# Attention and expert layer on one core: the rotary affine moved behind the rotation, and the prologue reordered

## The reference, cut to what matters

```python
xn = x / jnp.maximum(norm, EPS) * g
uv = jax.nn.silu(xn @ uv_w.T)
u, v, base = uv[..., :E], uv[..., E:2 * E], uv[..., 2 * E:]
base = base[:, :, None, :] * gamma[None, None] + beta      # two rows: q and k
base = _rope_seq(base)    # concat([x1*cos - x2*sin, x2*cos + x1*sin]) over halves of 64
q, k = base[:, :, 0], base[:, :, 1]
qk = jnp.einsum('bis,bjs->bij', q, k) + w_rel[idx][None]
kernel = jnp.square(jax.nn.relu(qk / sqrt_s))
out = u * jnp.einsum('bij,bje->bie', kernel, v)
```

## Time and profile before

| | us |
|---|---|
| median of the runs | 323.87 |
| the three runs | 323.11, 326.44, 323.87 |
| the profiled execution | 326.97 |
| its span (first to last instruction) | 323.7 |
| TensorE busy in the span | 311.1 (96%) |
| VectorE, ScalarE, GpSimd busy | 239.1, 219.7, 190.2 |
| mean granted TensorE clock | 0.989 of full |

### The profile page before, as it was taken

How to read it: one execution, slowest core, us unless ns; L and a number is a source line. 1 busy time by engine, 2 the same in 40 slices (tenths; PEclk the granted TensorE clock), 3 DMA queues, 4 the chain that set the end, 5 groups by cost and what they waited for, 6 DMA issues and landing times.

```text
span 323.7 us, 7700 instructions
## 1 busy us (share of the span) xinstructions
PE 311.1 (96%) x2041; PEld 249.8 (77%) x2041; DVE 239.1 (74%) x776; ACT 219.7 (68%) x439; POOL 190.2 (59%) x190
## 2 busy tenths in 40 slices
PE   8969799999999999999999899999999999999996
PEld 7736365665758566575747899988999999999995
DVE  4770838988897888889898778996455545487766
ACT  2739538588586858756164677768888888698751
POOL 5471607048687787848565577787775455455440
PEclk9979989999999999999999999999999999999999
DMA  6993420002111110211115313323333222573744
GB/s 185 275 287 118 139 67 25 7 0 69 33 49 48 38 42 25 67 34 57 43 40 127 77 58 115 104 82 110 107 105 89 77 70 75 182 244 98 231 129 130
DMA packets 40972, 31.20 MB, mean 96 GB/s; under 512 B 5675, under 2 KB 36960, under 8 KB 40932
## 3 DMA queue, kind: packets, MB, share of 16 engines
q1 hardware_dynamic: 35472, 21.88, 24.6%
q0 software_dynamic: 4192, 8.44, 7.4%
q10 hardware_dynamic: 1268, 0.40, 0.6%
HBM read 16.95 MB, written 11.88 MB: 89 GB/s over the span
## 4 chain that ended last, share of the span: by engine, by line
PE 68%; DVE 9%; DMA 8%; ACT 6%; issue 6%; SPq 1%; ACTq 0%; POOL 0%; DVEq 0%; POOLq 0%
PE B_o L884 16%; PE B_o L954 13%; PE B_uv L943 12%; PE B_S L866 6%; PE B_o L893 4%; DMA y<-u,xb 3%; ACT s_rel L666 3%; PE B_uv L856 3%; PE B_uv L848 3%; DVE K L1381 2%; PE B_m L909 2%; PE B_xT L840 2%; DVE t L1162 1%; DMA v<-y 1%; PE B_xT L832 1%
## 5 line engine op out<-in xcount | busy, mean ns | idle before, releaser
L578 POOL DMA_INDIRECT y<-u,xb x67 | 67.3, 1005 | 43.0 <-ACT u L708 32.8
L954 PE MATMUL B_o<-W2s,K 128*128 x568 | 75.9, 277 | 2.2 <-DVE K L1381 1.3
L537 POOL DMA_INDIRECT slots<-rows,pos x64 | 66.3, 1036 | 18.1 <-issue 17.2
L954 PEld LDWEIGHTS B_o<-W2s,K 128*128 128x128 f32 x568 | 69.0, 192 | 4.0 <-issue 3.8
L884 PE MATMUL B_o<-K,v 128*128 128x512 f32 x128 | 60.4, 607 | 0.0
L884 PEld LDWEIGHTS B_o<-K,v 128*128 128x128 f32 x128 | 23.8, 196 | 21.8 <-issue 21.3
L866 PE MATMUL B_S<-qk 128*128 128x512 f32 x64 | 35.4, 637 | 3.4 <-DVE qk L1176 2.4
L943 PE MATMUL B_uv<-xbT,t 128*128 128x128 f32 x288 | 38.0, 275 | 0.0
L697 ACT ACTIVATE t<-W1s 128x644 f32 x36 | 26.5, 739 | 13.9 <-DVE yd L1387 12.7
L943 PEld LDWEIGHTS B_uv<-xbT,t 128*128 128x128 f32 x288 | 35.0, 192 | 0.5 <-issue 0.5
L1381 DVE TENSOR_TENSOR K<-B_uv,t 128x512 f32<-128x512 f32 x36 | 24.7, 688 | 13.3 <-PE B_uv L943 13.1
(11 more groups left out here) (238 smaller groups left out, 642.7 us busy)
## 6 DMA issues: line engine op xcount, KB each, us to landing
xb<-slots SPq DMA_DIRECT2D x71, 65.0 KB, 1.9
x_all<-L_attn_x SPq DMA_DIRECT2D x8, 256.0 KB, 3.1
W1s<-L_ffn_W SPq DMA_DIRECT2D x1, 2048.0 KB, 9.1
rows<-rows SPq DMA_DIRECT2D x8, 256.0 KB, 2.6
x_all<-y SPq DMA_DIRECT2D x4, 512.0 KB, 4.5
out<-acc SPq DMA_DIRECT2D x7, 256.0 KB
y<-u,xb POOLq DMA_INDIRECT x67, 2.4
slots<-rows,pos POOLq DMA_INDIRECT x64, 2.3
```

The source lines that it names most:

```text
L537: pool.indirect_dma_start(out=slots, out_offset=bass.IndirectOffsetOnAxis(ap=pos[:, q % 2, c:c + 1], axis=0), in_=rows[:, q % 2, c // T, c ...
L578: pool.indirect_dma_start(out=y2, out_offset=bass.IndirectOffsetOnAxis(ap=xb[:, k, D:D + 1].bitcast(u32), axis=0), in_=yb[:, k, :], in_off ...
L954: last = nc.tensor.matmul(B_y[n % 2], hT[:, n % 2, c * P:(c + 1) * P], W2s[:, bass.ds(w + c * D, D)], start=(c == 0), stop=(c == T - 1))
```

## The change

The affine is taken through the rotation. With R(x) = near(x)*cos + far(x)*sin, where far swaps the halves of 64 features and the sign lies in the table: R(gamma*base + beta) = gamma * (base*cos) + gamma_far * (base_far*sin) + (beta*cos + beta_far*sin). The last term depends on no batch.

- ScalarE writes `base2` with two planes, the silu of `B_xT` and the silu of `B_xT` with halves swapped (two instructions of 64x512), straight out of PSUM; `scale_base` is gone. Batch 0 signals its first plane by itself (`base_ready`).
- VectorE makes `rope_beta` once (`far_affine`, `beta_sin`, `beta_cos`: two small copies and four instructions of 128x512). Per batch it does one product of both planes with `rope_tab`, whose planes are the two tables (128x1024), and four scalar_tensor_tensor of 128x512 (`rope_near`, `rope_far`), which take gamma as a per-partition scalar. GpSimd's share in batch 0 is gone; there `first_rope` does the product in two halves, the near part while ScalarE still writes the swapped plane.
- SyncE loads both tables, in two DMAs, ahead of `W2` of expert 0 and of x(1).
- `rs1` and `mr1` have two buffers, so that `ln1_pow(b)` and `ln1_apply(b)` wait for z of batch b - 2 instead of b - 1.
- In the prologue: `first_mean` after `weights_low`; `bias_window` ahead of `ln1_stats(1)`, both after the rotation of batch 0; `ln1_apply(2)` ahead of the rotation of batch 1; `first_norm(0)` after both silus of base and u; `squares(0, 2)` ahead of `scaled_x(1)`; `first_norm(1)` after `scaled_x(2)` and `first_norm(2)` last; `constant_rows` of expert 2 from ahead of `project_v(0)` to behind `scores(0)`.

The rows of an engine's order below give line (of its own kernel, so lines differ), operation, output, inputs, shape and count.

VectorE, batch 0, before: from the last copy of the transposed weights to the bias window `G`.

The diff, cut to its core:

```diff
-        cosT = sb("cosT", [P, L])
-        sinT = sb("sinT", [P, L])
+        gb_far = sb("gb_far", [P, 2, 2])
+        rope_tab = sb("rope_tab", [P, 2, L])
+        cosT, sinT = rope_tab[:, 0, :], rope_tab[:, 1, :]
+        rope_beta = sb("rope_beta", [P, 2, L])
...
-        rs1 = sb("rs1", [P, 2, T])
+        rs1 = sb("rs1", [P, 2, 2, T])
...
-        mr1 = sb("mr1", [P, T])
+        mr1 = sb("mr1", [P, 2, T])
...
-        base2 = sb("base2", [P, L])
-        gbase = sb("gbase", [P, 2, L])
+        base2 = sb("base2", [P, 2, L])
...
+                for table, ins in ((cosT, rope_cos), (sinT, rope_sin)):
+                    sp.dma_start(table, ins).then_inc(s_ld_rope, 16)
                 load_W2(0, 1, s_ld_w2_first)
                 load_x(1)
-                sp.dma_start(cosT[:, :], rope_cos).then_inc(s_ld_rope, 16)
-                for lo, hi in ((0, HALF), (HALF, 0)):
-                    sp.dma_start(sinT[lo:lo + HALF, :], rope_sin[hi:hi + HALF, :]).then_inc(s_ld_rope, 16)
                 load_W2(1, 3, s_ld_w2_next)
...
-            def first_cos():
-                pool.wait_ge(s_ld_rope, 48)
-                for k in range(2):
-                    pool.wait_ge(scaled, k + 1)
-                    last = pool.tensor_tensor(t1[:, k, :], gbase[:, k, :], cosT[:, :], ALU.mult)
-                last.then_inc(rope_step, 1)
-            def ln1_pow(b):
+            def ln1_pow(b, q):
                 pool.wait_ge(ln1_var, b + 1)
-                after(pool, z_ready, b)
-                pool.tensor_tensor(rs1[:, :, :], pw1[:, :, :],
+                after(pool, z_ready, b - 1)
+                pool.tensor_tensor(rs1[:, q % 2], pw1[:, :, :],
...
-            first_cos()
-            ln1_pow(1)
+            ln1_pow(1, 1)
             later_constants()
             pool.wait_ge(s_ld_rep, 16 * 2)
-            ln1_pow(2)
+            ln1_pow(2, 2)
...
-                    after(act, scaled, 2 * b)
+                    after(act, rope_step, ROPE * b - 1)
+                    base = nc.scalar.activation(base2[:, 0, :], B_xT[:, :], ACT.Silu)
+                    if b == 0:
+                        base.then_inc(base_ready, 1)
+                    for lo, hi in ((0, HALF), (HALF, 0)):
+                        far = nc.scalar.activation(base2[lo:lo + HALF, 1, :], B_xT[hi:hi + HALF, :], ACT.Silu)
+                    far.then_inc(silu_done, 1)
+                    return
                 if n == 1:
                     after(act, gated, b - 1)
                 if n == 2:
                     after(act, av_ps, b - 1)
-                o, ps = ((base2[:, :], B_xT), (u2[:, q % 2, :], B_uv),
-                         (v2[:, q % 2, :, :].rearrange("p t e -> p (t e)"), B_uv))[n]
-                nc.scalar.activation(o, ps[:, :], ACT.Silu).then_inc(silu_done, 1)
+                o = (u2[:, q % 2, :], v2[:, q % 2, :, :].rearrange("p t e -> p (t e)"))[n - 1]
+                nc.scalar.activation(o, B_uv[:, :], ACT.Silu).then_inc(silu_done, 1)
...
-            def scale_base(b):
-                after(act, s_ld_small, 0 if b else 32)
-                act.wait_ge(silu_done, 3 * b + 1)
-                after(act, rope_step, ROPE * b - 1)
-                for k in range(2):
-                    nc.scalar.activation(gbase[:, k, :], base2[:, :], ACT.Identity, bias=gb[:, 1, k:k + 1],
-                                         scale=gb[:, 0, k:k + 1]).then_inc(scaled, 1)
...
+            silu(0, 0, 0)
+            silu(0, 1, 0)
             first_norm(0, 0)
-            silu(0, 0, 0)
-            scale_base(0)
-            silu(0, 1, 0)
             silu(0, 2, 0)
             squares(0, 0)
             squares(0, 1)
+            squares(0, 2)
             scaled_x(1)
-            squares(0, 2)
             evac_xT(1, 1)
             squares(0, 3)
-            first_norm(1, 1)
             silu(1, 0, 1)
-            scale_base(1)
             silu(1, 1, 1)
             scaled_x(2)
-            first_norm(2, 2)
+            first_norm(1, 1)
             evac_xT(2, 2)
             silu(1, 2, 1)
             silu(2, 0, 2)
+            first_norm(2, 2)
             for n, p, a, r, q in pipeline(act):
-                if p is not None:
-                    scale_base(p)
...
-            constant_rows((1, 2))
+            constant_rows((1,))
             project_v(0, 0)
             scores(0)
-            constant_rows((3, 4))
+            constant_rows((2, 3, 4))
...
-            def ln1_apply(b):
+                stt(mr1[:, 0], mv1[:, :, 0], -1.0, rs1[:, 0, 0, :], ALU.mult, ALU.mult).then_inc(mr1_ready, 1)
+            def ln1_apply(b, q):
                 dve.wait_ge(ln1_rstd, b + 1)
-                after(dve, z_ready, b)
-                stt(mr1[:, :], mv1[:, :, 0], -1.0, rs1[:, 0, :], ALU.mult, ALU.mult).then_inc(mr1_ready, 1)
+                after(dve, z_ready, b - 1)
+                stt(mr1[:, q % 2], mv1[:, :, 0], -1.0, rs1[:, q % 2, 0, :], ALU.mult, ALU.mult).then_inc(mr1_ready, 1)
                 after(dve, xs_ready, T * b)
-                ts(rg[:, :], rs1[:, 1, :], g_col[:, :], None, ALU.mult).then_inc(rg_ready, 1)
+                ts(rg[:, :], rs1[:, q % 2, 1, :], g_col[:, :], None, ALU.mult).then_inc(rg_ready, 1)
...
-            def rope_cos(b):
-                dve.wait_ge(scaled, 2 * b + 2)
-                after(dve, rope_step, ROPE * b)
-                tt(t1[:, :, :], gbase[:, :, :], cosT[:, :].unsqueeze(1).broadcast_to(both),
-                   ALU.mult).then_inc(rope_step, 1)
-            def first_sin():
-                dve.wait_ge(s_ld_rope, 48)
+            def far_affine():
+                dve.wait_ge(s_ld_small, 32)
+                for lo, hi in ((0, HALF), (HALF, 0)):
+                    cp(gb_far[lo:lo + HALF], gb[hi:hi + HALF]).then_inc(beta_step, 1)
+            def beta_sin():
+                dve.wait_ge(beta_step, 2)
+                dve.wait_ge(s_ld_rope, 32)
                 for k in range(2):
-                    dve.wait_ge(scaled, k + 1)
-                    for lo, hi in ((0, HALF), (HALF, 0)):
-                        last = tt(t2[lo:lo + HALF, k, :], gbase[hi:hi + HALF, k, :], sinT[hi:hi + HALF, :], ALU.mult)
-                        if k == 1:
-                            last.then_inc(rope_step, 1)
-            def rope_sin(b):
-                after(dve, rope_step, ROPE * b)
-                dve.wait_ge(scaled, 2 * b + 2)
-                for lo, hi in ((0, HALF), (HALF, 0)):
-                    tt(t2[lo:lo + HALF, :, :], gbase[hi:hi + HALF, :, :],
-                       sinT[hi:hi + HALF, :].unsqueeze(1).broadcast_to([HALF, 2, L]), ALU.mult).then_inc(rope_step, 1)
-            def rope_sum(b):
+                    ts(rope_beta[:, k, :], sinT, gb_far[:, 1, k:k + 1], None, ALU.mult).then_inc(beta_step, 1)
+            def beta_cos():
+                for k in range(2):
+                    dve.wait_ge(beta_step, 3 + k)
+                    stt(rope_beta[:, k, :], cosT, gb[:, 1, k:k + 1], rope_beta[:, k, :], ALU.mult,
+                        ALU.add).then_inc(beta_step, 1)
+            def rope_near(b):
+                dve.wait_ge(beta_step, 6)
+                for k in range(2):
+                    last = stt(t2[:, k, :], t1[:, 0, :], gb[:, 0, k:k + 1], rope_beta[:, k, :], ALU.mult, ALU.add)
+                last.then_inc(rope_step, 1)
+            def rope_far(b):
+                after(dve, s_ps, 4 * b)
                 dve.wait_ge(rope_step, ROPE * b + 3)
-                after(dve, s_ps, 4 * b)
-                tt(qk[:, :, :], t1[:, :, :], t2[:, :, :], ALU.add).then_inc(rope_step, 1)
+                for k in range(2):
+                    last = stt(qk[:, k, :], t1[:, 1, :], gb_far[:, 0, k:k + 1], t2[:, k, :], ALU.mult, ALU.add)
+                last.then_inc(rope_step, 1)
+            def first_rope():
+                dve.wait_ge(base_ready, 1)
+                tt(t1[:, 0, :], base2[:, 0, :], cosT, ALU.mult).then_inc(rope_step, 1)
+                dve.wait_ge(rope_step, 1)
+                rope_near(0)
+                dve.wait_ge(silu_done, 1)
+                tt(t1[:, 1, :], base2[:, 1, :], sinT, ALU.mult).then_inc(rope_step, 1)
+                rope_far(0)
+            def rope_products(b):
+                dve.wait_ge(silu_done, 3 * b + 1)
+                dve.wait_ge(rope_step, ROPE * b)
+                tt(t1[:, :, :], base2[:, :, :], rope_tab[:, :, :], ALU.mult).then_inc(rope_step, 2)
+            def rope_sums(b):
+                dve.wait_ge(rope_step, ROPE * b + 2)
+                rope_near(b)
+                rope_far(b)
...
+            weights_low()
             first_mean()
-            weights_low()
+            far_affine()
+            beta_sin()
             xT_rest(0, 0)
+            beta_cos()
+            first_rope()
+            bias_window()
             ln1_stats(1)
-            first_sin()
-            rope_sum(0)
-            bias_window()
-            ln1_apply(1)
+            ln1_apply(1, 1)
             ln1_stats(2)
             xT_rest(1, 1)
-            rope_cos(1)
```

(13 more changed lines are left out.)

18 lines of the change are left out of this document (8 added, 10 removed).

## The result

| us | before | after |
|---|---|---|
| median of four runs each, same chip | 324.07 | 319.03 |
| lowest and highest | 323.11, 326.44 | 318.19, 321.91 |
| profiled execution, its span | 326.97, 323.7 | 318.65, 316.9 |
| scores of batch 0, 1, 7 start at | 19.59, 48.89, 161.03 | 17.29, 41.80, 154.98 |

The medians lie 5.0 us apart. The ratio is 0.9857 with a 95% interval of 0.9818 to 0.9897, so 4.6 us faster, 3.3 to 5.9 by the interval. The forecast was 317.7, a gain of 6.2. The last line of the table cuts the gain up: 2.3 us are won before the first scores, 7.1 before the scores of batch 1, and one of them is given back by batch 7. Every ratio here leaves out executions in a slower state of the chip, in which the same kernel takes some per cent longer; every median is over all executions.

What follows compares the result with a forecast made beforehand. TensorE, busy 96% of the span, was taken as the bound, with time to win only in the prologue. 1.7 + 1.5 + 1.86 + 1.7 - 0.4 - 0.15 = 6.2 us, from the median 323.87 to 317.7; range 315.3 to 320.7.

Steps and rivals of the forecast that it cites:

- The two stalls: Prologue: TensorE idle 2.43 us before batch 0's scores and 1.86 us from 36.80, each followed by a lower clock.
- Term 1: Rotation of batch 0: scores start 6.0 us after the base projection, idle 0.7 instead of 2.43, 1.7 us gained.
- Term 2: Work put ahead of the base projection: xT_rest(0) starts 0.1 to 0.7 us later, 0.4 us lost.
- Terms 3 and 4: Clock stays full after the first stall, 1.5 us gained; second stall goes, 1.86 gained plus 1.7 for its clock.
- Term 4's cause: Second stall: xs of batch 2 waits for mrg, behind rope_cos(1), 2.06 us, and a four-element instruction of 1.22 us.
- Term 5: Entry to the loop: ScalarE starts the first relu some 0.15 us late, bounds 0 and 0.5; lost once.
- The loop: TensorE bounds each pass, so shorter VectorE or ScalarE work gains nothing; the pass stays 18.76 us.
- rival C: Loop: GpSimd blocks the new two-input sums, 4.8 us a pass if in full; 331 us, chance 0.03.
- A: Before batch 0's scores: the clock falls in the 0.7 us gap after all, costing 1.5; 319.2 us, chance 0.12.
- B: Prologue: tables land late, projection 1.9 us late, clock falls, 1.5 + 1.5 lost more; 320.7 us, chance 0.08.
- D: Second stall stays in part, GpSimd's constants or roots taking longer; some 2 us, 319.7 us, chance 0.07.
- low end of the range: Whole kernel: Term 2 and Term 5 at nothing, a shorter idle, and the median wandering by a us: 315.3 us.

Runs made afterwards that it cites:

- run 2: The kernel before, unedited, profiled again on another chip: 355.12 us.
- run 5: Changed kernel with two extra 1024-column VectorE products, results unread, ahead of the last sums of batch 0: 352.14 us.
- run 4: Kernel before with only the second stall's cure (two buffers, later waits, z moved, columns of batch 2 ahead of the cosine product): 356.46 us, ratio 0.9882 to before.
- run 10: Changed kernel with two 512-column GpSimd products, results unread, beside the rotation of batch 0: 349.81 us, one execution.
- run 8: The kernel of run 7 with GpSimd's z product in the loop behind two instead of four indirect DMAs: 348.77 us, ratio 0.9855 to before.
- run 7: Changed kernel with z of batch 2 moved into ScalarE's gap ahead of the v silu of batch 1: 350.46 us, ratio 0.9836 to before.
- 12: The kernel of run 8 once more, on the third chip, beside the changed kernel: 348.43 us, ratio 0.9835 to before.
- run 1: The changed kernel again, unedited, beside before on another chip: 350.01 us, ratio 0.982 to before.
- run 3: Changed kernel with the second stall's causes put back (z order, waits for z, columns of batch 2 behind batch 1's product): 353.72 us, ratio 0.9925 to before.
- run 9: Changed kernel with both table loads put back behind W2 of expert 0 and x(1): 346.81 us, one execution.

## Why the prediction was right, and where it was off

**The two stalls** (what bounds the kernel now): right. Both falls of the clock come again in run 2; run 5 makes the first by hand in the changed kernel, run 4 takes the second away in the old one. Without the waits the clock is full.

**Term 1**, idle 2.43 to 0.7, scores at 17.3: they started at 17.29, with 0.29 idle. The rows of the chain were right to 0.1, silus of 64 partitions cost what 128 cost (0.60 each), and what made room was GpSimd's absence (run 10). The idle time is smaller than forecast for two reasons: the chain took 5.85 us from the projection instead of 6.0, and TensorE's own work 5.56 (11.44 to 17.00) instead of 5.3. Expert 2's rows are 8 of 16 products there, not four of eight; the half is right.

**Term 2**, 0.4 lost: `xT_rest` started at 10.61 instead of 10.07, so 0.54. The two tensor_scalar took 0.88 against 1.0. W2's first piece landed at 10.1, not 9.5, and TensorE waited 0.72 for it; its products still ended 0.18 before the projection. The forecast cover was just enough.

**Terms 3 and 4**, 1.5 and 1.86 + 1.7: right in kind, and the second stall is worth more than that. TensorE's timeline of before, on from the earlier trace rows, and ScalarE's `xs` of batch 2:

```profile
39.99 5.13 PE L884 MATMUL B_o<-K,v 128*128 128x512 f32 x8
44.56 2.00 PE L856 MATMUL B_uv<-uvT,xT 128*128 128x256 f32 x12
```

```profile
38.02 1.65 ACT L639 ACTIVATE xs<-x_all,mrg,rg 128x128 f32<-128x128 f32 x4 [3.90 <-DVE mrg L1141]
```

The same marks of both kernels cut up the time between the scores of batches 0 and 1:

| stretch, us | before | after | saved | forecast |
|---|---|---|---|---|
| scores of batch 0 | 5.68 | 4.49 | 1.19 | 1.5 |
| up to the wait for `xs` of batch 2 | 11.53 | 12.26 | -0.73 | -0.95 |
| wait, transposition, half of `attend(0)` | 7.76 | 3.47 | 4.29 | 3.56 |
| up to the scores of batch 1 | 4.33 | 4.29 | 0.04 | 0 |
| sum | 29.30 | 24.51 | 4.79 | 4.11 |

The third line is where the terms were too small. Behind the wait of 1.86 the transposition in before takes its four inputs at ScalarE's pace: 1.33 us up to the next product instead of 0.43, at a granted clock of 0.99 up to 39.68. These 0.90 us are part of the stall, and the forecast had them at nothing. The clock then costs 1.53 (4.57 us instead of 3.04 for the half of `attend(0)`), not 1.7. By its own terms the forecast puts the scores of batch 1 at 42.5 and not at 42.7; they came at 41.8.

**Term 4's cause** holds one thing that the forecast read past. The instruction of 1.22 us that it names has four columns; five others of its line took 0.15 or 0.16. It ran beside GpSimd's product for the residual (34.31 to 36.43), and the one other that took long, 1.24, beside GpSimd's `z`. That is the meeting of run 8, and it was in the rows of before.

**Term 5**, 0.15 lost at the entry to the loop: mis-sized. It was 0.44 + 0.17 of waits for `s_rel`, 0.7 in the pass (run 7). ScalarE takes 3.38 us from its silu of base (40.43) to the first squares (43.81), and took 2.67 before, 0.52 of them idle. The forecast's own sizes, 3.7 us of work against 2.7 of work and idle time, would have given 1.0 and not 0.15.

**The loop**, "nothing gained": wrong in sign. By the scores' marks 7.1 us of gain at batch 1 are 6.05 at batch 7. Of the 1.04 lost, 0.65 is term 5 and 0.59 the pass of batch 5, 19.45 us against 18.86; the others win back 0.2. It is not the blocking of the new sums that the forecast's rival C feared. Their view in after, 48 to 156 us, near sums (least, median, longest in ns), the far ones alike:

```profile
L1155 DVE SCALAR_TENSOR_TENSOR t<-t,gb,rope_beta x12: 743/749/753, 50.0 to 145.0; 128x512 f32<-128x512 f32 x12
```

None is held up. It is rival C's mechanism at another place: `lm`. In after it takes 0.65, 0.74 and 0.83 us in three passes that lose nothing (18.72, 18.71, 18.72), and 0.92 instead of 0.32 in the one that does. There VectorE's chain behind it ends 0.6 later than in before, and TensorE has a product, which the three other passes lack, that waits for it:

```profile
136.68 0.27 PE L911 MATMUL B_m<-selcum,ones_r 128*128 128x8 f32 x1 [0.36 <-DVE rows L1267]
```

That this pass would be as short as before's without the hold-up is argued, not shown: in runs 8 and 12, where `lm` keeps 0.20, the same pass takes 19.4 and 19.5, with other waits. In run 1, on another chip, passes of 19.2 to 20.0 us, in which TensorE waited three times 0.3 for `go`, hold `lm` times of 1.31 to 1.47.

**Rivals.** A didn't come: gaps of 0.29, 0.63 (run 3) and even 1.73 (run 9) left the clock full, those of 2.2 to 2.6 (runs 2, 4, 5, 10) brought it down, and so did the one of 1.84 in before, behind which TensorE went on at ScalarE's pace. TensorE: Matmul & The Clock Gate of the Trainium skill (what's actually happening) puts it on recent load rather than on one gap; 1.73 harmless and 1.84 not, at different places, agrees with that and does not prove it. B would have been cheap: the table's lateness cost 0.65, not 3, as it gave W2 its place back and the clock stayed. D didn't come. C's price was mis-sized: the product of 1024 columns is two of 512, so that all blocked in full would be 5.8 us a pass and not 4.8.

**The sum**: 6.2 forecast; 6.05 by the scores of batch 7; 6.8 by the spans of the two profiled executions; 5.0 by the medians on that chip, 7.5 and 8.1 on two others (by the ratios 4.6, 6.4 and 8.9). Forecast and marks agree, and all medians lie on the same side. That they agree to 0.2 is in part luck: 0.7 more was won up to batch 1 than the terms say, and 1.04 lost behind it where they have 0.15. The low end of the range would be 315.6 by its own terms, not 315.3. Which part of the scatter among the medians is the chip's and which is chance, these runs do not tell.
